# A graph network on one core: gathers in pairs, held for VectorE's adds and for the queries' evictions

## The reference

```
q = (h @ Wq.T + bq)[dst]; k = (h @ Wk.T + bk)[src]; v = (h @ Wv.T + bv)[src]
alpha = sum(q * k) / sqrt(16)                     # per edge and head
a = exp(alpha - segment_max(alpha, dst)[dst]) / segment_sum(...)[dst]
out = segment_sum(a * v, dst)
```

## Time and profile before

| | us |
|---|---|
| median of 3 runs | 5614.84 |
| lowest, highest | 5613.83, 5617.6 |
| span of the profiled execution | 7840.1 |

### The profile page before, as it was taken

One profiled execution on the slowest core, in us unless ns is written; L12 is line 12 of the kernel. 1 busy time (PEld: TensorE's weight loads), 2 busy tenths in 40 slices (PEclk: granted clock), 3 DMA queues, 4 the chain that ended last, 5 costly groups with the idle time before them and its releaser, 6 DMA issues.

```text
span 7840.1 us, 106032 instructions
## 1 busy us (share of the span) xinstructions
PE 4625.7 (59%) x22831; PEld 3727.9 (48%) x22832; DVE 4037.4 (51%) x11107; ACT 2769.9 (35%) x6493; POOL 3849.3 (49%) x4066
## 2 busy tenths in 40 slices
PE   4555555655556556555555565555555656666667
PEld 2444444534444445344444453444444545555555
DVE  4555555645555556455555565555555553333334
ACT  1333333423333334233333342333333432323333
POOL 3555555335555553345555543455555425555553
PEclk6666666676666666766666667666666677877887
DMA  5222222222322222222223222222322211111111
GB/s 127 78 79 76 77 76 78 52 66 73 79 78 77 78 80 56 69 67 79 76 78 79 78 62 69 68 78 77 80 78 79 60 33 43 44 44 44 44 44 30
DMA packets 267188, 536.13 MB, mean 68 GB/s; under 512 B 116253, under 2 KB 148689, under 8 KB 266509
## 3 DMA queue, kind: packets, MB, share of 16 engines
q0 software_dynamic: 180992, 490.24, 23.6%
q1 hardware_dynamic: 78901, 35.89, 1.9%
q10 hardware_dynamic: 6936, 6.69, 0.3%
HBM read 512.41 MB, written 18.03 MB: 68 GB/s over the span
## 4 chain that ended last, share of the span: by engine, by line
PE 26%; another core or an unknown queue 26%; issue 20%; DVE 17%; ACT 5%; DVEq 4%; ACTq 1%; SPq 0%; DMA 0%; POOL 0%; POOLq 0%
PE bank L806 9%; PE bank L825 7%; DVE acc L1265 6%; ACT oh L556 2%; DVEq L333 2%; PE bank L797 2%; PE bank L851 2%; PE bank L810 1%; DVE alpha L1288 1%; PE bank L879 1%; DVEq L1265 1%; DVE slots L1361 1%; DVE oh L1249 1%; PE bank L1001 1%
## 5 line engine op out<-in xcount | busy, mean ns | idle before, releaser
L508 POOL DMA_INDIRECT slots<-kv_table,idx x3224 | 3065.2, 951 | 3133.0 <-PE bank L825 1275.8
L825 PE MATMUL bank<-slots,oh 128*128 128x136 f32 (+1 forms) x8060 | 1593.0, 351 | 569.1 <-DVE acc L1265 506.4
L806 PE MATMUL bank<-qs,ohT 128*128 x8080 | 1685.7, 356 | 235.1 <-ACT ohT L547 129.2
L825 PEld LDWEIGHTS bank<-slots,oh 128*128 128x128 f32 x8060 | 1411.7, 252 | 704.7 <-DVE acc L1265 608.2
L806 PEld LDWEIGHTS bank<-qs,ohT 128*128 128x128 f32 x8080 | 1434.4, 257 | 456.6 <-issue 434.4
L1265 DVE TENSOR_TENSOR acc<-acc,bank 128x136 f32 (+1 forms) x4030 | 1172.0, 291 | 614.6 <-PE bank L825 171.5
L1282 DVE TENSOR_TENSOR slots<-slots,bank 128x512 f32<-128x512 f32 x808 | 551.8, 683 | 1322.6 <-remote 1291.5
L547 ACT ACTIVATE ohT<-bank,miss 128x512 f32<-128x512 f32 x1010 | 676.7, 683 | 1367.9 <-PE bank L797 1234.5
L508 POOL DMA_INDIRECT slots<-src_table,idx x806 | 760.4, 943 | 756.9 <-DMA idx<-src_e 247.9
L843 PE MATMUL bank<-ident,alpha 128*128 128x128 f32 x204 | 93.7, 459 | 1487.2 <-DVE alpha L1288 1481.7
L556 ACT ACTIVATE oh<-iota,rel_e 128x128 f32<-128x128 f32 x3168 | 962.8, 387 | 0.0
(11 more groups left out here) (257 smaller groups left out, 4079.5 us busy)
## 6 DMA issues: line engine op xcount, KB each, us to landing
slots<-kv_table,idx POOLq DMA_INDIRECT x3224
kv_table<-slots SPq DMA_DIRECT2D x20, 660.0 KB, 3.4
slots<-src_table,idx POOLq DMA_INDIRECT x806
resets<-flat_len ACTq DMA_DIRECT2D x51, 128.0 KB
idx<-src_e SPq DMA_DIRECT2D x255, 8.0 KB
terms<-flat_rel SPq DMA_DIRECT2D x255, 12.0 KB
resets<-flat_rst SPq DMA_DIRECT2D x2, 1551.0 KB
w<-in_w SPq DMA_DIRECT2D x8, 256.0 KB
```

The lines of the kernel that those rows point to most:

```text
L508: pool.indirect_dma_start(slots[:, k, t, 0:width], None, table, bass.IndirectOffsetOnAxis(ap=idx[:, k, t:t + 1], axis=0))\
L806: mm = pe.matmul(o, ohT[:, j % 2, t, :], qs[:, blocks[j * G + t], 0:HID], start=True, stop=basis is None)
L825: mm = pe.matmul(bank[6 + part % 2][:, o:o + width], oh[:, k % 2, t, :], slots[:, k, t, HID:HID + width], start=True, stop=True)
```

## The change

Three things. `START` goes from 13 to 80. Before each group of gathers in the four layers GpSimd also waits until VectorE has evicted a number of blocks of queries: two for each group that has gone before in the ring (chunk k, group j: 2(4k + j), at most 25); in later turns of the ring the count is long reached. And before places 2, 4, 6 to 14 of each chunk it waits for `acc_done` to reach the count at which VectorE has added the place before in the chunk four back; a register `added` carries the count.

```
-START = (RING - 1) * NG + 1
+START = (RING + 1) * CH
+PACE = 2
...
+            added = pool.alloc_register("added")
+            pool.reg_mov(added, PACE)
...
                 for j in range(groups):
+                    if l is not L:
+                        pool.wait_ge(q_ev, START + NB * l + min(NB, 2 * (NG * k + j)))
                     if isinstance(turn, int):
                         pool.wait_ge(slot_free[k][j], START + turn)
                     else:
                         pool.wait_ge(slot_free[k][j], START + used[j])
                         pool.reg_add(uses[k][j], uses[k][j], 1)
                     for t in range(j * G, min((j + 1) * G, places)):
+                        if t % PACE == 0 and t > 0:
+                            after_next = t + PACE if t + PACE < places else CH + PACE
+                            before = pool.snap(added)
+                            if isinstance(turn, int):
+                                pool.wait_ge(acc_done, START + CH * (L * CHUNKS + RING * FULL + k - RING) + t)
+                            else:
+                                pool.wait_ge(acc_done, START - CH * RING + before)
+                            pool.reg_add(added, added, after_next - t)
                         pool.indirect_dma_start(slots[:, k, t, 0:width], None, table,
```

## The result

| kernel | runs | median us | lowest to highest |
|---|---|---|---|
| before, on the same chip | 10 | 5617.83 | 5613.83 to 9772.95 |
| after | 10 | 5632.2 | 5628.18 to 5647.04 |

The ratio is 1.0028, with a 95% interval of [1.0019, 1.0037]: slower by 14.4 us in the medians, 16 us by the ratio. The one run of before at 9772.95 us is left out of the ratio. It spans 5645.2 us, 0.2% over the median.

The account below looks back on a forecast made before the run. GpSimd's stream of gathers was taken to bound all five phases; layer 0's hold adds 12 us and everything else 0, so 5614.8 + 12 = 5627 us, +0.2%, with a range of 5550 to 5670 (the forecast's own 5615 to 5640).

Parts of the forecast that it names:

- The bound: All five phases: GpSimd's stream of gathers sets the time, 20.0 us a chunk against 18.9 for the chunk's own chain.
- That layer 0 pays it all: Layer 0: gathers need 1048 us, the chain 1034, so the 14 us margin makes it pay the whole stop.
- The sum of the kernel before: Whole kernel before: gathers, layer ends, restarts, start and end together 5592.6 us, 22 us under the median.
- The hold in layer 0: Layer 0's head: the fifth gather waits for the second eviction, 15.2 to 15.6 us standing; net cost 12, between 11 and 15.5.
- up to 2.6 us for an earlier reload: Layer 0's head: with no gathers running, VectorE's reload may land after 3.4 us instead of about 6, shortening the stop.
- Holds in layers 1 to 3: Heads of layers 1 to 3: evictions run ahead of the groups that wait for them, cost 0.
- Pairs' waits and their instructions: All five phases: the 1760 added waits find adds long done, and their register operations lie under the gathers; cost 0.
- The constant: Start value of all counting semaphores, from 13 to 80: same instructions, cost 0.
- Rival two: Layer 0: the hold is hidden by earlier evictions or a chain of 19.2 or more; no change, 5615 us; chance 0.20.
- Rival three: GpSimd's sequencer: the new waits' register operations add to the stream, +221 us, 5836 us; chance 0.08.
- Rival one: Late TensorE signals are partly real and the holds remove a third of the lateness: about 5530 us; chance 0.22.
- the 1.7 us delay of a chunk's third group: Chunks with the ring full, as in the profile: the third group waits for place 7's add, 1.7 us later, cost 0.

Follow-up runs that it names:

- fewer gathers: Kernel before without gathering place 15 of chunks 4 to 49 of each phase, 230 of 4030 gathers, all arithmetic kept: 5479.65 us, ratio 0.9752.
- before once more: The kernel before, unchanged, in a second profiled execution: one timed run of 5615.54 us, profiled span 5613.7 us.
- hold alone: Kernel before with the new START and the gathers' wait on the queries' evictions, no waits on adds: 5635.53 us, ratio 1.0026.
- second and fourth experiments: Second: waits on adds without the evictions' hold, 5621.05 us, ratio 1.0001. Fourth: changed kernel with PACE 1 instead of 2, 5634.24 us, ratio 1.0026 to before.
- wait before every place: Changed kernel with PACE 1 instead of 2, a wait before each place but a chunk's first: 5634.24 us, ratio 1.0026 to before.
- pairs' waits alone: Changed kernel's register `added` and waits on `acc_done`, without the evictions' hold: 5621.05 us, ratio 1.0001 to before.
- layer 0 exempt: Changed kernel with the queries' hold taken out of layer 0 only, GpSimd's layer loop peeled: 5619.95 us, ratio 1.0005 to before.

## Why the prediction was right, and where not

**The bound: right, on a thinner margin than I thought.** The stream of gathers sets the time in the message phase and in layers 1 to 3 (57.4 us and 17 to 39 us came off when it was shortened). My 18.9 us for the chain of a chunk was too small: 19.5 in layer 1 and 19.6 in layers 0 and 2. I took it from six periods at the ends of layers, and the ends are quicker than the rest. The kernel with fewer gathers shows it behind layer 1's last gather, where no gather sets the pace:

```profile
2134.11 0.48 DVE L1347 TENSOR_TENSOR_SCAN fwd<-resets,icol,bank 128x128 f32<-128x128 f32 x1 [1.06 <-issue]
...
2152.79 0.48 DVE L1347 TENSOR_TENSOR_SCAN fwd<-resets,icol,bank 128x128 f32<-128x128 bf16 x1 [1.12 <-issue]
...
2171.40 0.48 DVE L1347 TENSOR_TENSOR_SCAN fwd<-resets,icol,bank 128x128 f32<-128x128 bf16 x1 [0.88 <-issue]
```

These are 18.7 and 18.6 apart, in a layer whose mean is 19.5. The first to the last add of a phase that is not held by its stream gives the mean.

**That layer 0 pays it all: right, with luck.** From the first gather to the last add of layer 0 I had 1034 us by the chain and 1048 by the gathers. The kernel with fewer gathers, whose chain sets the pace there, took 1053.9, the kernel before once more 1054.5. So the margin of 14 us was about 1. By my own condition (a chain of 19.2 or more) the stop would have been hidden. It was not, because the sum by gathers was 6.5 us too small as well and the chain's head too long: the first multiplication comes 48.5 us behind the first gather, not 53.8. With the hold the chain also starts later: the first add comes 73 to 74 us behind the first gather in after and in the hold alone, and 68 in the kernels with no hold in layer 0. So a somewhat slower chain would have hidden a part of the stop and not all of it; no kernel here shows how much.

**The sum of the kernel before: right, with one term too small.** It came out 22 us short. Measured in before once more, the four stretches from a layer's last gather to its last add are 43 to 44 us, 173.7 in all, where I had 38.2 and 152.8. That is 21 of the 22; the other terms are off by 6 us at most each and cancel.

**The hold in layer 0: right place, term too small.** Forecast 12 (11 to 15.5); the kernels with it cost 14.4 to 15.7. The stop was nearly as worked out: 15.2 to 15.6 of standing was the forecast, 14.95 and 15.28 were read. The 1.4 us of slow gathers did come back: no gather of 1.48 us or more is left behind the first. The term that was mis-sized is the up to 2.6 us for an earlier reload. VectorE stood 4.08 us for it in after:

```profile
66.26 1.09 DVE L1653 TENSOR_TENSOR oh<-oh 128x896 f32<-128x896 f32 x1 [4.08 <-DMA oh<-flat_dst]
...
72.19 0.75 DVE L1478 TENSOR_TENSOR qs<-bank,vec_qs 128x256 f32<-128x256 f32 x2
```

and 4.83 in before once more, against 5.26 in the earlier trace rows. Over all profiled executions it stood 4.04 to 4.55 us in the four kernels with the hold in layer 0 and 4.57 to 5.26 in the six executions without, 0.6 us less in the mean. So with the gathers stopped beside it the reload came about half a microsecond sooner, not 2.6. A restart also takes longer, 0.84 to 0.99 us from the end of the eviction to the start of the gather (72.94 to 73.92 in after), where I had 0.3 to 0.7. Stop less slow gathers is 14.95 - 0.30 - 1.4 = 13.3 (13.6 with the hold alone). The last 1 to 2 us up to the timed difference I can't assign; they are within the interval. The evictions are not faster either: all 25 from first to last start take 16.2 us after (72.2 to 88.4) and 15.9 before (71.8 to 87.7). The hold frees nothing.

**Holds in layers 1 to 3: right.** The gathers of layer 1 take 1009.0 us in before once more (1178.6 to 2187.6) and 1008.8 with the hold alone (1194.6 to 2203.4). After took 1011.9 (1194.7 to 2206.6), since its gathers were 3 ns longer in that execution (median 949 ns against 946). With still more waits they were at 946, so this is the execution and not the waits; 4030 x 0.003 = 12 us is most of the 15 that this execution lies above the median.

**Pairs' waits and their instructions: right**, by the second and fourth experiments. When the last gather of layer 0 goes out in after, 26 adds are still to come, the same as in before once more at the end of layer 1; a pair asks for an add 65 places back. I had called this distance about a chunk; it is nearer two.

**The constant: right.**

**The rivals.** Rival two (no change) is outside the interval, which begins at 1.0019. Rival three (the waits' instructions add up to 221 us) is refuted by the wait before every place: 2000 more waits, no more time. Rival one (faster, 0.22) is refuted too. In the profile of before once more GpSimd's gathers run back to back and no signal is late. VectorE's multiplication that waited 7.43 us follows at once there:

```profile
2605.28 0.28 DVE L1265 TENSOR_TENSOR acc<-acc,bank 128x136 f32 x1
2605.48 0.68 DVE L1282 TENSOR_TENSOR slots<-slots,bank 128x512 f32<-128x512 f32 x1
```

This also takes down a sentence of mine: that signals come late while gathers run back to back "and not otherwise". It was true inside that one execution, and I took it for a property of the kernel. From it came the one plain miss, the profiled span "within about 2% of 7840": it was 5645.2. And the 1.7 us delay of a chunk's third group was never seen, as it needs a full ring. The forecast of the time survived because the sum was set against the timed runs and took only what the first profile showed in stretches without late signals.

The Trainium skill (Perfetto Trace Analysis, § GPSIMD Engine Instruction) tells to use start-to-start spacing for GpSimd, and the traces agree: by the recorded 0.946 us a gather a chunk would be 15.1 us and shortening it would have brought nothing, by the spacing of 1.25 the message phase had to lose 57.5 and lost 57.4.

**No better version came out.** The pairs' waits alone and layer 0 exempt equal the kernel before and don't beat it. The fewer gathers show what a cheaper stream would be worth: 1 to 39 us a layer, since the chain follows close behind it; in the message phase the 1.25 us per chunk were gained in full. I have no way to gather the same rows with fewer gathers, and tried none.

## What to carry to other kernels

The stream of gathers runs without slack here, and it paid every stop that was tried, in layer 0 and in the later layers. Such a hold is free only where what it asks for has already happened, so ask for each of its places when that is (here 15 us late in layer 0, early in all others). To learn whether a stream is the bound, shorten the stream alone and read each stage's gain: it tells the distance to the next limit too, which no share of busy time does. And when a profile is much longer than the timed runs, compare stages with a second execution before taking a mechanism from it.

## What the runs showed of the hardware

- **One execution that is far longer.** The kernel before took 7840.1 us in its first profiled execution and 5613.7 in its second. In the first, VectorE's multiplication stood 1291.5 us on a sender without name; in before once more VectorE has no such wait. The mean granted clock in the middle of layer 1 differed as well. The two, first and once more, in a stretch of layer 1: its length, the busy time of TensorE's matmuls and weight loads, VectorE, ScalarE and GpSimd with their instructions, the granted clock, the DMA share and GB/s:

```profile
1700.00:2900.00 1200.00, 679.44 (x3285) 550.10 (x3286) 650.09 (x1770) 431.80 (x1098) 632.74 (x666) 0.63 0.29 76
```

```profile
1200.00:2100.00 900.00, 687.47 (x3585) 566.21 (x3586) 701.95 (x1933) 471.51 (x1203) 681.24 (x719) 0.73 0.41 110
```

  The clock is the lower because TensorE had longer pauses, or the pauses are longer because of the clock; the traces don't tell. What draws an execution out like that stays open. It does not come with the lack of the hold alone: four kernels without the queries' hold in layer 0, before itself among them, had spans of 5613.7 to 5622.2 us.
- **An indirect gather of 128 rows starts 1.25 us after the last, at either length of its rows**: 1009.0/805 = 1.253 us with 1056 B, 1005.9/805 = 1.250 us with 512 B. Waits and register operations between two of them are not seen, one wait per gather included.
- **The granted clock goes with the pace of the chain.** In layers 1 to 3 of the kernel with fewer gathers it was 0.75 to 0.78 in the mean, against 0.73 in before once more, and its adds of layer 3, at 0.78, took 969.3 us against 982.8 and 986.0 at 0.76 and 0.75. Which of the two follows the other isn't shown. So the chain's 19.5 us a chunk are not a fixed number, and that they would be the same beside the full stream isn't shown either.
